# A Flamingo block with two mixture-of-experts layers: the order of the routed tiles, their first rows, the idle shares and the weight blocks rearranged

## The chip, the cores and the metric

The kernel runs on one core of a Trainium2 chip. The metric is the device time of one execution in microseconds (us), the median of several runs; less is better. Engine names: PE is TensorE's matmuls and PEld its weight loads, DVE is VectorE, ACT is ScalarE, POOL is GpSimd, SP is SyncE, which here only issues DMAs.

## The reference, cut to what matters

`x` is 4 x 256 tokens of 256 numbers, so N = 1024 tokens. Four steps follow each other, each with a residual.

```python
x = x + tanh(g_xattn[0]) * L0_xattn(layernorm(x), ctx)          # fp8-quantised product
x = x + tanh(g_ffn[0])   * L0_ffn(layernorm(x), ...)            # 8 small experts, top 2, and a shared one
x = x + tanh(g_xattn[1]) * L1_xattn(layernorm(x), ctx, ctx)     # 16 heads, causal
x = x + tanh(g_ffn[1])   * L1_ffn(layernorm(x), ...)

def L1_ffn(x, rw1, rw2, w1, b1, w2, b2):                        # TOP_K = 2, E = 8, hidden 1024
    probs = softmax(gelu(x @ rw1) @ rw2)
    wgt, idx = top_k(probs, 2)
    for e in range(E):
        Ye = gelu(x @ w1[e] + b1[e]) @ w2[e] + b2[e]
        Ce = gelu(b1[e]) @ w2[e] + b2[e]                        # what a token gets that did not choose e
        for k in range(2):
            mask = idx[..., k] == e
            active = any(mask)
            out = out + active * wgt[..., k] * where(mask, Ye, Ce)
```

The last step holds most of the arithmetic. A token needs `Ye` only for its two experts; for the others it gets a weighted sum of the constant rows `Ce`. The kernel calls that sum the idle share.

## The kernel before, in words

The program is written by hand for each engine: one instruction list per engine, with semaphores between them. Every list runs in order, so an instruction that waits holds up all that stands behind it on its engine. The stages are A (first attention product), B (first expert layer), C (second attention, four batches b = 0 to 3 with twelve pieces u each) and D (second expert layer).

**Weight blocks.** The weights of stage D (`w1`, `w2`, eight experts each) come in 32 blocks of 128 x 1024 numbers, two per expert and matrix, in the order of the list `ORDER`. SP loads block i into staging buffer i % 4 once `s_wlo` says that block i - 4 is done. ACT scales it (L828) and writes its 16-bit high part (L835); POOL then subtracts to get the low part, in four pieces (L663), and raises `s_wlo`. These conversions are laid by hand between the work of stages B to D: `C_BLOCKS` and `SCALE_AT` say which block is scaled at which piece u of stage C (the high part follows at u + 1), `D_BLOCKS` are those left for stage D (blocks 21 to 31; `D_BLOCKS[-2:]` have their low part made by DVE, L2120).

**SP's list in stage C.** Between the loads stand the small DMAs of `load_minus_max(b)` (L516), the rows without which PE cannot begin `scores_by_key(b, 0)` (L1329). `load_minus_max(3)` stands behind the load of block 20.

**Routing.** DVE takes the two largest logits of each token (L2039, L2045), PE counts with matmuls how many tokens before this one chose the same expert, DVE adds up where each expert's run of slots begins, each padded to 128, and makes for each pair (token, choice) a one-hot row of its slot (sixteen instructions, L2080). PE turns them into the list of tokens by slot, DVE stores it as indices (`GI`, `SI`, L2092 to L2094), POOL gathers the rows of a tile from DRAM by them (`gather_rows`, L721).

**Tiles.** There are TILES = 23 tiles of 128 slots. For a tile j: PE transposes its gathered rows (L1528), DVE copies them (`rows_t`, L2127), PE multiplies with the expert's `w1` (`tile_up`, L1544 and L1547, four PSUM banks), DVE adds the halves (`add_halves`, four L2159), ACT does gelu and the high part (L1063, L1070), DVE the low part (`split_hidden`, two L2164), PE multiplies with `w2` (`tile_down`, L1562 and L1565, which stands in the list after `tile_up(j + 1)`), ACT and DVE weight the result (L1078, `tile_out` L2169), POOL adds the rows into DRAM with an indirect accumulating DMA (`add_to_out`, L734). Each `add_to_out` waits until the one before has landed (`s_sc`), and stands in POOL's list behind the gather of tile j + 4, which waits until ACT has copied the row weights of tile j + 2 (`s_ws`, L1057). The expert of a tile is a number read at run time (`EID`); SP copies its `w1` within SBUF into one of three buffers `W1S` (L564) for each tile.

**Idle shares.** PE forms all `Ce` (`idle_outputs`, L1488, 64 matmuls before tile 0 and 64 behind `tile_up(0)`), folds them (L1507), and multiplies with the tokens' coefficients (`idle_shares`, L1516) behind `tile_up(1)`; DVE adds that to X (L2146), SP stores X to `out`, and only then may `add_to_out(0)` run.

## Time and profile before

| what | us |
|---|---|
| median of 3 runs | 435.31 |
| lowest and highest | 434.76 and 436.42 |
| profiled execution, its own time | 430.72 |
| its span, first to last instruction | 428.8 |
| busy in the span: PE, DVE, ACT, POOL | 319.6, 307.7, 262.0, 166.6 |
| mean granted TensorE clock, share of full speed | 0.898 |

The profile is of one execution, whose time is 4.6 us below the median of the timed runs. All times of instructions are from the beginning of its span. A line of a timeline has the start, the duration (of all its instructions together where it ends on xN), engine, line, operation, what is written from what, and in brackets the idle time ahead of it with the engine and line that ended it.

### The profile page before, as it was taken

How to read it: one execution, taken by the hardware profiler on the slowest of the kernel's cores; microseconds unless marked ns; L12 is line 12 of the kernel's file. 1: busy time of each engine (PE TensorE's matmuls, PEld its weight loads, DVE VectorE, ACT ScalarE, POOL GpSimd, SP SyncE). 2: the span in 40 equal slices, each digit the busy share in tenths (PEclk: the TensorE clock that was granted, in tenths of full speed). 3: DMA queues.
4: the chain of work that ended last, by engine and by line, in shares of the span. 5: the costliest groups of instructions: out<-in, count | busy, mean ns of one | idle time of the engine just before them, and what ended most of it. 6: DMA issues, size and time to landing. Idle time of an engine off the chain costs nothing.

```text
span 428.8 us, 8535 instructions
## 1 busy us (share of the span) xinstructions
PE 319.6 (75%) x2638; PEld 216.0 (50%) x2639; DVE 307.7 (72%) x739; ACT 262.0 (61%) x528; POOL 166.6 (39%) x231
## 2 busy tenths in 40 slices
PE   0065988869999968777582511578999999999981
PEld 0054337536477635354341210365777777777760
DVE  3998988863764666759676689466788788888870
ACT  1745656623576476848687598033677777777770
POOL 3041301531284260623671659200355444444422
PEclk9997799989999998979788565678999999999997
DMA  8954000140076073411313535834477777777532
GB/s 265 389 144 136 2 0 2 53 142 2 0 165 233 2 208 72 141 50 51 99 50 99 159 92 147 315 130 171 149 247 248 246 245 245 236 248 233 157 36 24
DMA packets 28097, 60.43 MB, mean 141 GB/s; under 512 B 4401, under 2 KB 19010, under 8 KB 24866
## 3 DMA queue, kind: packets, MB, share of 16 engines
q1 hardware_dynamic: 21186, 52.64, 35.6%
q0 software_dynamic: 4416, 6.13, 8.9%
q10 hardware_dynamic: 2464, 1.27, 1.2%
q8 instruction: 16, 0.26, 0.3%
q14 instruction: 15, 0.12, 0.1%
HBM read 27.43 MB, written 6.32 MB: 79 GB/s over the span
## 4 chain that ended last, share of the span: by engine, by line
DVE 36%; PE 32%; issue 11%; ACT 11%; DMA 4%; POOL 3%; ACTq 1%; DVEq 0%; POOLq 0%
PE bank L1202 6%; PE bank L1544 4%; PE bank L1562 4%; ACT arena L1063 4%; DVE MX L1902 4%; DVE arena L2080 2%; PE bank L1547 2%; PE bank L1163 2%; DVE X L1748 2%; ACT arena L1070 2%; DVE arena L2164 2%; DVE arena L2159 2%; PE bank L1565 2%; DVE stats L1626 2%; ACT arena L945 2%
## 5 line engine op out<-in xcount | busy, mean ns | idle before, releaser
L1063 ACT ACTIVATE arena<-arena,B1D 128x128 f32<-128x128 f32 x184 | 57.6, 392 | 14.3 <-DVE arena L2159 13.7
L1562 PE MATMUL bank<-arena 128*128 x184 | 62.3, 385 | 1.2 <-DVE arena L2164 1.2
L2159 DVE TENSOR_REDUCE arena<-bank 128x256 f32<-128x512 f32 x92 | 57.4, 683 | 4.6 <-PE bank L1547 4.6
L663 POOL TENSOR_TENSOR arena<-STG,arena 128x256 f16<-128x256 f32 x56 | 37.1, 695 | 42.4 <-ACT arena L835 42.4
L663 POOL TENSOR_TENSOR W<-STG,W 128x256 f16<-128x256 f32 x64 | 41.4, 683 | 28.3 <-ACT W L835 28.3
L1565 PE MATMUL bank<-arena 128*128 x184 | 50.7, 276 | 0.0
L734 POOL DMA_INDIRECT out_dram<-arena,SI x23 | 37.3, 1621 | 31.0 <-DMA out_dram<-arena,SI 23.7
L721 POOL DMA_INDIRECT arena<-token_rows,GI x23 | 22.8, 991 | 66.5 <-ACT WS L1057 51.3
L2164 DVE SCALAR_TENSOR_TENSOR arena<-arena 128x512 f16<-128x512 f32 x46 | 29.8, 689 | 24.8 <-ACT arena L1070 24.8
L1544 PE MATMUL bank<-arena 128*128 128x256 f16 x256 | 46.4, 281 | 1.5 <-DVE arena L2127 1.1
L1547 PE MATMUL bank<-arena 128*128 128x128 f16 x256 | 45.4, 225 | 0.0
L945 ACT ACTIVATE arena<-bank 128x512 f32<-128x512 f32 x48 | 27.9, 595 | 22.6 <-PE bank L1332 22.4
L1202 PE MATMUL bank<-arena 128*128 128x256 f32 x160 | 38.8, 395 | 0.5 <-issue 0.5
L828 ACT ACTIVATE STG<-STG 128x1024 f32<-128x1024 f32 x32 | 33.5, 1047 | 6.4 <-DMA STG<-in_l_w_dram 5.0
L1902 DVE TENSOR_REDUCE MX<-bank 128x2 f32<-128x512 f32 (+1 forms) x48 | 31.2, 687 | 8.6 <-PE bank L1304 8.1
L633 POOL TENSOR_TENSOR rstd<-ve,neg_half 128x2 f32<-128x2 f32 (+1 forms) x12 | 9.7, 807 | 68.8 <-DVE ve L1631 68.8
L1202 PEld LDWEIGHTS bank<-arena 128*128 128x128 f32 x160 | 30.4, 196 | 5.5 <-issue 1.5
L1163 PE MATMUL bank<-arena 128*128 128x512 f16 x120 | 31.3, 405 | 0.0
L1544 PEld LDWEIGHTS bank<-arena 128*128 128x128 f16 x256 | 25.8, 101 | 7.5 <-DVE arena L2127 1.3
L1562 PEld LDWEIGHTS bank<-arena 128*128 128x128 f16 x184 | 18.2, 99 | 21.9 <-issue 3.4
L876 ACT ACTIVATE arena<-bank,B1A 128x512 f32<-128x512 f32 x20 | 13.6, 686 | 24.0 <-PE bank L1163 20.1
L1070 ACT ACTIVATE arena<-arena 128x512 f16<-128x512 f32 x46 | 26.1, 613 | 0.0
(266 smaller groups left out, 708.5 us busy)
## 6 DMA issues: line engine op xcount, KB each, us to landing
STG<-in_l_w_dram SPq DMA_DIRECT2D x32, 512.0 KB, 3.6
arena<-W SPq DMA_DIRECT2D x16, 1024.0 KB, 5.0
STG<-W SPq DMA_DIRECT2D x7, 1024.0 KB
arena<-in_l_w_dram SPq DMA_DIRECT2D x2, 1280.0 KB, 12.2
X<-in_x_dram SPq DMA_DIRECT2D x2, 512.0 KB, 6.1
W<-in_ctx_t_dram ACTq DMA_DIRECT2D x2, 512.0 KB, 11.2
W<-in_ctx_dram SPq DMA_DIRECT2D x1, 1024.0 KB, 17.6
k_parts<-W SPq DMA_DIRECT2D x2, 512.0 KB, 3.3
```

Source lines behind the costliest of these rows:

```text
L663: ins = nc.gpsimd.tensor_tensor(l, src, h, ALU.subtract)
L734: pool.indirect_dma_start(out[:, :], bass.IndirectOffsetOnAxis(ap=SI[:, j:j + 1], axis=0), YS[:, j % 2], None, compute_op=ALU.add).then_in ...
L1063: ins = nc.scalar.activation(x, x, ACT.Gelu, bias=B1D[:, e, c:c + 1], scale=1.0 / (X_SCALE * W_SCALE))
L1163: mm = nc.tensor.matmul(bank[UP_BANK[i]][:, :], W1A[:, b, c, k], HT_[:, k, a, h * 512:(h + 1) * 512], start=(n == 0), stop=(n == 5))
L1202: nc.tensor.matmul(dst, GH[:, c, t * P:(t + 1) * P], W2A[:, c], start=(c == 0), stop=False, skip_group_check=True)
L1544: nc.tensor.matmul(o, W1S[r][:, 0, k, c * P:(c + 1) * P], XT[:, q, k].rearrange("p s n -> p (s n)"), start=(k == 0), stop=False, skip_grou ...
L1547: mm = nc.tensor.matmul(o[:, 0:P], W1S[r][:, 1, k, c * P:(c + 1) * P], XT[:, q, k, 0], start=False, stop=(k == KC - 1), skip_group_check=True)
L1562: nc.tensor.matmul(bank[6 + q][:, :], GDL[:, q, 0, c * P:(c + 1) * P], W2[:, e, c].rearrange("p s d -> p (s d)"), start=(c == 0), stop=Fal ...
L1565: mm = nc.tensor.matmul(bank[6 + q][:, 0:D], GDL[:, q, 1, c * P:(c + 1) * P], W2[:, e, c, 0], start=False, stop=(c == HC8 - 1), skip_group ...
L1902: v.tensor_reduce(MX[:, b % 2, i, h0:h0 + nh], s1_bank[n % 2][:, :].rearrange("p (h n) -> p h n", h=nh), AX.X, ALU.max).then_inc(s_mx, 1)
L2159: v.tensor_reduce(half, o, AX.X, ALU.add).then_inc(s_dadd, 1)
L2164: v.scalar_tensor_tensor(out=lo, in0=GD[:, q, hb * 512:(hb + 1) * 512], scalar=G_SCALE, in1=hi, op0=ALU.mult, op1=ALU.subtract).then_inc(s ...
```

## The change

- The first eight tiles are one per expert, in the fixed order `STATIC` = 4, 5, 6, 7, 0, 1, 2, 3. An expert's first 128 tokens go there, whatever the others have; only tokens beyond go to tiles 8 to 22, whose experts are still read at run time. Tiles 0 to 7 take `w1` where it lies, without a copy. All loops over tiles are written out.
- The rows of tiles 0 and 1 are not gathered: DVE makes one-hot rows for them from the rank alone, and PE multiplies them with the rows in SBUF, which gives them transposed. Their gathered rows are still fetched, for the row weights.
- `idle_outputs`, coefficients, fold and `idle_shares` move to behind tiles 6 to 13, with their copies on ACT. X is stored early (`store_base`), and the idle shares are added to `out` by one accumulating DMA of 1 MB (`add_shares`) between `add_to_out(15)` and `add_to_out(16)`. Weighted rows have ten buffers: three for tiles 0 to 15 in turn, and one each for tiles 16 to 22.
- A new order of the weight blocks: ACT splits blocks 4 to 7 before `hidden_gelu(CA)` of stage B; stage C takes blocks 12 to 23, three per batch; blocks 24 to 28 come in stage D before the routing, 29 to 31 after it, with their low parts on POOL between the tiles.

```diff
-        HEAD, UNROLL = 3, 6
+        ONE_HOT = 2
+        STATIC = [*range(E // 2, E), *range(E // 2)]
...
-        C_BLOCKS = [range(10, 13), range(13, 16), range(16, 19), range(19, 21)]
-        SCALE_AT = ((1, 4, 8), (2, 5, 8), (2, 5, 8), (2, 5))
-        D_BLOCKS = range(21, BLOCKS)
+        C_BLOCKS = [range(12, 15), range(15, 18), range(18, 21), range(21, 24)]
+        SCALE_AT = ((5, 8, 10), (2, 5, 8), (2, 5, 8), (2, 5, 8))
+        LATE = 29
+        SHARES_AFTER = 15
+        def weighted(j):
+            return YS[j % 3] if j <= SHARES_AFTER else YS[3 + j - SHARES_AFTER - 1]
+        def added(j):
+            return 16 * (j + 1 + (j > SHARES_AFTER))
...
@@ SP
             load_minus_max(2)
-            for i in range(18, 21):
+            for i in range(21, 25):
                 load_weights(i)
             load_minus_max(3)
...
+            def store_base(h):
+                sp.wait_ge(s_dhs, HT * (h + 1))
+                sp.dma_start(out[h * HT * P:(h + 1) * HT * P, :].rearrange("(t p) d -> p t d", p=P),
+                             X[:, h * HT:(h + 1) * HT, :]).then_inc(s_out, 16)
@@ POOL
-            weights_low(4)
-            pool.wait_ge(s_up, 2 * CA)
-            for i in range(5, 10):
+            for i in range(4, 12):
                 weights_low(i)
...
+            def add_shares(n):
+                pool.wait_ge(s_share, T)
+                pool.wait_ge(s_sc, 16 * n)
+                pool.dma_start(out[0:N, :].rearrange("(t p) d -> p t d", p=P), X[:, :, :],
+                               accum_op=ALU.add).then_inc(s_sc, 16)
...
-            for j in range(4):
+            for j in (2, 0, 3, 1, 4):
                 gather_rows(j)
             for j in range(TILES):
-                if j + 4 < TILES:
-                    gather_rows(j + 4)
+                if j + 5 < TILES:
+                    gather_rows(j + 5)
                 add_to_out(j)
+                if j == SHARES_AFTER:
+                    add_shares(j + 1)
+                if j == 3:
+                    pool.wait_ge(s_gb16, 2)
+                if 3 <= j < 3 + BLOCKS - LATE:
+                    weights_low(LATE + j - 3)
@@ ACT
+            for i in range(4, 8):
+                weights_split(i)
             hidden_gelu(CA)
...
+            def one_hot_rows_out(j):
+                act.wait_ge(s_xt_ps, j + 1)
+                nc.scalar.activation(XT[:, j]..., bank[j][:, :], ACT.Copy).then_inc(s_xt, 1)
+            one_hot_rows_out(0)
+            weights_split(29)
+            one_hot_rows_out(1)
+            for i in range(30, BLOCKS):
                 weights_split(i)
@@ PE
+            def one_hot_rows(j):
+                pe.wait_ge(s_oh, j + 1)
+                for k in range(KC):
+                    for s in range(2):
+                        for t in range(T):
+                            mm = nc.tensor.matmul(bank[j][:, (2 * k + s) * P:(2 * k + s + 1) * P],
+                                                  DHL[:, t, s, k * P:(k + 1) * P], OH[:, j, t], ...)
+                mm.then_inc(s_xt_ps, 1)
...
+            for j in range(ONE_HOT):
+                one_hot_rows(j)
+            for j in range(TILES):
+                e = expert_of(j)
+                tile_up(j, e)
+                if j == 0:
+                    slot_tokens()
+                if 4 <= j + 1 < TILES:
+                    transpose_tile(j + 1)
+                if j:
+                    tile_down(j - 1, e_before)
+                if j in (1, 2):
+                    transpose_tile(j + 1)
+                if j in (6, 7):
+                    transpose_coefficients(j - 6)
+                if j == 8:
+                    idle_outputs()
+                if j == 9:
+                    fold_groups()
+                if j in (10, 11, 12, 13):
+                    idle_shares(2 * (j - 10))
@@ DVE
+            step(v.scalar_tensor_tensor(out=RANK1[:, :, :], in0=rank[:, :, ones_hot], scalar=1.0,
+                                        in1=MSB[:, :, ones_hot], op0=ALU.add, op1=ALU.mult))
+            def one_hot_rows(j):
+                v.tensor_tensor(OH[:, j], iota_1[:, :].unsqueeze(1).broadcast_to([P, T, P]),
+                                RANK1[:, :, j:j + 1].broadcast_to([P, T, P]), ALU.is_equal).then_inc(s_oh, 1)
+            one_hot_rows(0)
...
+            slots_out()
+            for j in range(TILES):
+                add_halves(j)
+                if ONE_HOT <= j + 1 < TILES and j > 2:
+                    rows_t(j + 1)
                 for hb in range(2):
-                    split_hidden(j, j % 2, hb)
+                    split_hidden(j, hb)
+                if j in (1, 2):
+                    rows_t(j + 1)
                 if j:
-                    tile_out(j - 1, (j - 1) % 2)
+                    tile_out(j - 1)
+                if j == 2:
+                    tile_experts()
+                if j == 3:
+                    coefficients()
+                if j == 4:
+                    spread_gelu()
```

## Rows read from the trace of the kernel before

**Rows 1.** The page: the chain that ended last, its shares by engine.

```profile
DVE 36%; PE 32%; issue 11%; ACT 11%; DMA 4%; POOL 3%; ACTq 1%; DVEq 0%; POOLq 0%
```

**Rows 2.** Stretches: length; busy PE, PEld, DVE, ACT, POOL; clock; DMA share; GB/s.

```profile
149.00:161.60 12.60, 8.88 (x116) 5.36 (x116) 7.69 (x21) 9.19 (x17) 7.34 (x11) 0.94 0.66 179
...
207.60:232.70 25.10, 14.58 (x144) 8.37 (x140) 16.68 (x47) 19.76 (x30) 10.45 (x16) 0.84 0.34 101
...
307.00:410.00 103.00, 103.00 (x986) 80.14 (x983) 83.29 (x152) 77.54 (x227) 47.63 (x37) 1.00 0.73 229
```

**Rows 3.** Timeline of DVE from the router's logits to the slots.

```profile
249.09 0.68 DVE L2039 MAX8 DTOP<-bank 128x8 f32<-128x8 f32 x8 [0.55 <-PE bank L1447]
...
256.59 10.06 DVE L2080 TENSOR_SCALAR arena<-iota_p,SMODF,token 128x128 f16<-128x128 f16 x16
...
268.29 0.18 DVE L2094 SCALAR_TENSOR_TENSOR SI<-bank,arena 128x23 uint32<-128x23 f32 x1
...
270.74 2.35 DVE L2120 TENSOR_TENSOR arena<-STG,arena 128x1024 f16<-128x1024 f32 x2
```

**Rows 4.** Timeline of DVE: instructions beside a busy and an idle POOL.

```profile
110.96 0.15 DVE L1638 TENSOR_TENSOR rt<-ve,rstd 128x2 f32<-128x2 f32 x1
...
111.74 0.74 DVE L1886 TENSOR_SCALAR W<-X,mv,rstd 128x256 f32<-128x256 f32 x2
...
237.32 1.40 DVE L1943 TENSOR_SCALAR arena<-X,mv,rstd 128x256 f32<-128x256 f32 x2
```

**Rows 5.** Timeline of POOL: low parts of weight blocks, four pieces a block.

```profile
115.51 2.55 POOL L663 TENSOR_TENSOR W<-STG,W 128x256 f16<-128x256 f32 x4 [10.38 <-ACT W L835]
...
203.38 5.16 POOL L663 TENSOR_TENSOR arena<-STG,arena 128x256 f16<-128x256 f32 x8
```

**Rows 6.** Timelines of ACT and DVE in batch 0 of stage C.

```profile
150.71 1.05 ACT L835 ACTIVATE W<-STG 128x1024 f16<-128x1024 f32 x1
...
158.40 1.56 DVE L1893 TENSOR_TENSOR W<-W 128x256 f16<-128x256 f32 x2 [3.01 <-ACT W L912]
```

**Rows 7.** Timelines of SP and PE where batch 3 begins.

```profile
201.75 1.32 SPq L516 DMA_DIRECT2D arena<-NMS  x2
...
207.59 0.40 PE L1329 MATMUL bank<-ident_b,neg_mask 128*128 128x256 bf16 x1
...
213.58 1.09 PE L1360 MATMUL bank<-ident,arena 128*128 128x128 f32 x4 [3.77 <-DVE arena L1932]
```

**Rows 8.** Timelines of PE (transposes at a low clock) and DVE (one tile).

```profile
183.01 1.04 PE L1280 MATMUL bank<-ident_h,W 128*128 128x128 f16 x8 [1.76 <-DVE W L1893]
...
302.49 2.47 DVE L2159 TENSOR_REDUCE arena<-bank 128x256 f32<-128x512 f32 x4
...
306.35 1.29 DVE L2164 SCALAR_TENSOR_TENSOR arena<-arena 128x512 f16<-128x512 f32 x2 [1.05 <-ACT arena L1070]
...
307.95 2.48 DVE L2159 TENSOR_REDUCE arena<-bank 128x256 f32<-128x512 f32 x4
```

**Rows 9.** Idle outputs in PE's timeline, idle shares in the chain.

```profile
283.41 1.93 PE L1488 MATMUL bank<-arena 128*32 128x256 f16 x64
...
295.22 2.31 PE bank L1516 x8
```

**Rows 10.** Timelines of DVE (tile 17) and POOL (adds of tiles 15, 21, 22).

```profile
384.84 2.48 DVE L2159 TENSOR_REDUCE arena<-bank 128x256 f32<-128x512 f32 x4
...
387.79 1.59 POOL L734 DMA_INDIRECT out_dram<-arena,SI  x1 [0.72 <-issue]
...
418.64 1.55 POOL L734 DMA_INDIRECT out_dram<-arena,SI  x1 [3.04 <-DVE arena L2169]
423.27 1.55 POOL L734 DMA_INDIRECT out_dram<-arena,SI  x1 [3.08 <-DMA out_dram<-arena,SI]
```

**Rows 11.** Waits: who waited for whom, total, times, longest.

```profile
ACT WS L1057 <- DVE arena L2169: 22.1, 21, 1.4
```

**Rows 12.** DMA queue in the last 10.2 us: packets, MB, share of 16 engines.

```profile
q0 software_dynamic: 288, 0.26, 24.1%
```

585 lines of the change are left out of this document (292 added, 293 removed).

## The prediction

> **What bounds the kernel now.** I read the page's chain of waits first. It is shared: DVE 36%, PE 32%, ACT 11% [rows 1], so no engine alone sets the time, and each stage has to be read for itself. The view of busy times by stretch cuts it. In the loop over tiles, 307 to 410 us, PE is busy for all 103 us at full clock, DVE for 80.14 [rows 2]: PE is the bound, and a tile takes 307.95 - 302.49 = 5.46 us [rows 8]. Before it stands a chain of latencies, seen in DVE's timeline: logits at 249.09, sixteen one-hot rows from 256.59 (10.06 us, 0.63 each), the indices done at 268.5 [rows 3], then gathers, transposes, tile 0, idle outputs, idle shares, and the first reduction of tile 3 only at 307.95 [rows 8]. The end is a third regime: POOL's adds wait for the one before to land, 423.27 - 418.64 = 4.63 us apart, and the span ends 5.53 after the last one's issue [rows 10]. In stages B and C, ACT, PE and DVE hand work round, and none is full: ACT is busy 9.19 of 12.60 us in the second half of batch 0 and 19.76 of 25.10 in batch 3 [rows 2].
>
> The profiled span is 428.8, that execution's own time 430.72, the median 435.31. I add the change of the span to the median. The sum has four terms: up to tile 3, extras in the loop, slips in stages B and C, the tail.
>
> **Term 1, up to tile 3: -23.4.** Routing stays where it is up to the ranks. After the last logit (249.1) DVE makes masks, rank and the product RANK1, about as many small instructions as it now does in that time: about 253. The one-hot rows of tile 0 are one instruction on 1024 elements; the nearest price is 2.35/2 = 1.17 us [rows 3], plus some 0.5 because POOL still makes low parts then: 254.8. PE multiplies 32 times at 0.13, the price of the transposes with a slow clock (8 in 1.04) [rows 8]: about 258.5 with its wait. ACT copies, so `tile_up(0)` begins near 261.5 and ends near 264.1. Under this cover DVE makes the second tile's rows (1.2), the slots (thirteen small ones, about 3), and the sixteen one-hot rows for all slots. These took 0.63 each beside a working POOL [rows 3]. DVE instructions are shorter beside an idle one: 0.74 for two `scaled_q` against 1.40 [rows 4]; the shortest small one took 0.15 [rows 4]. POOL has no work here, as its gathers wait for the indices: I take 0.2 each, 3.2 in all, with 0.15 and 0.63 as ends. That puts the slots' end near 264, the indices near 265.5, and the first reduction of tile 0 at 265.5, because it stands behind the indices on DVE. ACT's splits of blocks 29 to 31 end near 266.4 and delay gelu little. From a first reduction to the end of the split a tile takes 306.35 + 1.29 - 302.49 = 5.15 [rows 8]: tile 0 is done at 270.8, tile 1 at 276.1, and with the copy of tile 2's rows (0.4) and its up product (1.1) tile 2 starts at 277.7. Rows are gathered five ahead, so no gather is late. Tile 3 starts at 277.7 + 5.15 + 1.6 = 284.5 instead of 307.95. The idle shares, which separated these tiles, are gone from here, and with them the wait of the first add for the store of X.
>
> **Term 2, extras in the loop: +10.0.** What leaves the front comes back where PE is full. `idle_outputs` cost 1.93 for 64 matmuls, and there are two sets: 3.9. The shares cost 2.31 [rows 9], the fold about 0.6: together 6.8, all on the bound. The coefficients' transposes go to tiles where DVE is late and cost nothing. DVE gets the tiles' experts, the coefficients and the spread of gelu, 3.6 by their count of small instructions, and POOL's low parts of three blocks (2.55 each [rows 5]) stretch DVE's work beside them by up to 0.47 of their time: 7.65 x 0.78 x 0.47 = 2.8. Of these 6.4 the idle time of DVE, (103 - 80.14)/103 x 5.46 = 1.2 per tile [rows 2], over six tiles, can swallow all, if it lies in the right place; I take half, +3.2, with 0 and 6.4 as ends. The W1 copies of tiles 0 to 7 go; they were on no path.
>
> **Term 3, slips in stages B and C: +5.2.**
> (a) POOL's low parts of blocks 4 to 7 move ahead of its wait for stage B's up products and fill a gap of 10.38 us before 115.51 [rows 5]. DVE's `ln_rstd` and `scaled_q` lie in it (four at 0.15, two in 0.74) [rows 4] and stretch by 0.5 and 0.66; PE's maxima wait for them: +1.2, ends 0 and 2.4 (both halves of the rows).
> (b) In batch 0 ACT's six half conversions stand at pieces 5 to 11 instead of 1 to 9, three more in the second half, 1.05 each, in a stretch where DVE once waits 3.01 for ACT [rows 6]. ACT has 3.4 us idle there [rows 2], but in pieces: half of 3.15 is paid, +1.5, ends 0 and 3.15.
> (c) SP's `load_minus_max(3)` is issued at 201.75 now; after, it stands behind the load of block 24, which waits for the low part of block 20, the last of POOL's two blocks from 203.38 (5.16): 208.5 [rows 5]. With issue (1.32 for its two) and landing PE could begin `scores_by_key(3, 0)` near 212.9 instead of 207.59 [rows 7]. PE has 3.77 us of idle time soon behind that [rows 7], which covers part: 5.3 - 3.8 = +1.5, ends 0 and 2.5.
> (d) Batch 3 gets one more block, 2.1 on ACT, of whose 5.3 idle us [rows 2] not all can be used: +1.0, ends 0 and 2.1.
> At nothing: the splits of blocks 4 to 7 ahead of stage B's gelu (ACT is idle there and gelu is used some 5 us later), the early store of X (SP, behind the token rows), five gathers ahead, static experts (fewer register loads, on queues that wait anyway). If ACT's cover in stage B is gone, a split costs 2 us each.
>
> **Term 4, the tail: +5.7.** Now: from the first reduction of tile 17 (384.84) to the end are 43.96 us, with the add of tile 15 issued 2.95 later, at 387.79 [rows 10]; the row weights' wait for `tile_out` [rows 11], which ten buffers remove, is part of that. After: add 15 at +1.3, 4.63 for its landing, then `add_shares`, D, then six gaps of 4.63, then 5.53: 39.2 + D. Behind this 1 MB transfer stand on POOL adds 16 to 22 and gathers 21 and 22. No row shows a transfer of this kind and size. Its floor is one add, 4.63. Two adds of 128 KB used 24.1% of 16 engines over 10.2 us [rows 12], 1.23 us of all engines each; eight times that is 9.8, and with the fixed 3.4 of an add 13.2. Direct rows should be somewhat cheaper than indirect ones: D = 10.5, so 49.7 - 43.96 = +5.7. The tail is as long as now at D = 4.7. The other six buffers only let ACT and DVE run ahead.
>
> **Sum.** -23.4 + 10.0 + 5.2 + 5.7 = -2.5: span 426.3, time 435.3 - 2.5 = 432.8 us. Most of the gain at the front is paid back in three other places, so the sum is small beside its terms.
>
> **Rivals.** 0.5%, or 2.2 us, is about what a measurement can tell from no change.
> 1. The share add is short (faster). Only its landing counts, and at D = 4.7 term 4 is zero: 432.8 - 5.8 = 427.1. For it: two adds in the tail leave 16 engines three quarters idle [rows 12], so an add's time is mostly latency, not data. Against: eight times the packets. Chance 0.19. The Trainium skill's page "DMA: Bandwidth & Descriptors", section "Anatomy of one DMA - SWDGE (gpsimd) path", is on this rival's side: it gives a GpSimd transfer a fixed 2.0 us plus its bytes at 436 GB/s, an estimate of 4.4 us for 1 MB; by it the sum would be rival 1's. No row of before has a transfer of this size with accumulation; the indirect adds' 4.63 for 128 KB is above the page's 2.3.
> 2. ACT and POOL find room for all moved conversions (faster): term 3 is zero, 427.6. For it: ACT has idle time in each batch [rows 2]. Against: DVE's wait for ACT in batch 0 [rows 6]. Chance 0.10.
> 3. They find none: term 3 is at its upper ends, 10.1, so 437.7. Chance 0.13.
> 4. The share add is long (slower). An indirect add keeps POOL for 1.59 us to build 128 rows' descriptors [rows 10]; eight times as many is 12.7, and if the data follow partly behind, D is 16 (landing alone behind) to 25, say 20: +9.5, 442.3. It makes the kernel slower from D = 10.5 + 2.5 + 2.2 = 15.2. For it: nothing can pass it, as the next add waits for its landing. Against: plain rows need no index each. Chance 0.15.
> 5. The early tiles don't come early, because the sixteen one-hot rows stay at 0.63 (not POOL but their form was what cost): 16 x 0.43 = +6.9, 439.7. Chance 0.11.
> My forecast holds 0.32.
>
> **How the numbers follow.** The likeliest is the sum, 432.8. Its own range is 429 to 436.5. The wanted range takes in rivals 1 and 2 (427) with half of the other small terms, and rivals 3, 5 and the lower half of 4: 425.5 to 443. Outside are rivals 1 and 2 together and a share add over 20 us. Faster by over 0.5%: rivals 1 and 2 (0.29) and the half of the forecast below 433.1 (0.17): 0.46. Slower: 4, 5 and half of 3: 0.32. Same: 0.22.
>
> **What would show it.** From the last logit to the first reduction of tile 3 should take 35.5 us instead of 58.9, the sixteen one-hot rows about 3 instead of 10. From tile 3 to tile 15 there should be about 10 us more than thirteen times 5.46. PE's first scores of batch 3 should begin 5 us later after its predecessor, and DVE should wait longer for ACT in batches 0 and 3. The gap between POOL's adds 15 and 16 should be 4.6 + 10.5, the later adds 4.63 apart. I am wrong if tile 3 still waits for DVE's slots (term 1), if the loop stays at 5.46 per tile with the extras in it (term 2), if the router's logits come no later than 249 (term 3), or if the gap around the share add is under 10 or above 20 us (term 4).

## The result: slower, by what was lost ahead of the router

The changed kernel takes 440.34 us (median of 4 runs, 439.03 to 441.44) against 435.03 for the kernel before in the same session: ratio 1.0125, 95% interval 1.0072 to 1.0178. Ratios are taken over the fast runs of each kernel, those within 1.5% of its fastest, so below they are not always the quotient of the medians. The forecast was 432.8, faster; the time lies in the forecast's range and on the other side. The profiled span grew from 428.8 to 437.3, by 8.5 us, while the medians are 5.3 apart: the profiled execution of before was a short one (430.72 against its median of 435.03), the one of the changed kernel less so (439.03 against 440.34). The 8.5 is nearer to what is usual: in two later groups the kernel before had medians of 430.94 and 431.12, and the nearest stand-ins for the changed kernel, e1 and e5 below, 440.71 and 440.43, with ratios of 1.027. The working below is on the two spans.

Four markers cut both traces where the forecast cut them.

| stretch | before | changed | difference | forecast |
|---|---|---|---|---|
| start to the router's logits (first MAX8) | 249.09 | 258.36 | +9.3 | +5.2 |
| logits to the first reduction of tile 3 | 58.86 | 33.17 | -25.7 | -23.4 |
| tile 3 to tile 17 | 76.89 | 91.26 | +14.4 | +10.0 |
| tile 17 to the end | 43.96 | 54.51 | +10.5 | +5.7 |
| span | 428.8 | 437.3 | +8.5 | -2.5 |

From the logits to the end the change is worth 0.8 us (179.7 against 178.9). What it gains at the first tiles is paid back, all but 0.8 us, by the loop and the tail, and what it loses in stages B and C is the loss.

The page's chain that ended last, where DMA has risen from 4% [rows 1] to 15%:

```profile
PE 31%; DVE 30%; DMA 15%; ACT 12%; issue 8%; POOL 2%; SPq 0%; ACTq 0%; DVEq 0%; POOLq 0%
```

DVE of the changed kernel from the logits to tile 3. L2200 are the sixteen one-hot rows (L2080 of before), L2256 a tile's reductions (L2159), L2262 the split's low parts (L2164).

```profile
258.36 0.68 DVE L2136 MAX8 DTOP<-bank 128x8 f32<-128x8 f32 x8 [0.55 <-PE bank L1528]
...
261.82 1.56 DVE L2160 TENSOR_TENSOR arena<-iota,RANK 128x1024 f16<-128x1024 f16 x1
...
269.01 3.65 DVE L2200 TENSOR_SCALAR arena<-iota_p,SMODF,token 128x128 f16<-128x128 f16 x16
...
273.48 2.47 DVE L2256 TENSOR_REDUCE arena<-bank 128x256 f32<-128x512 f32 x4
...
285.02 2.57 DVE L2256 TENSOR_REDUCE arena<-bank 128x256 f32<-128x512 f32 x4 [0.64 <-PE bank L1652]
...
291.53 2.57 DVE L2256 TENSOR_REDUCE arena<-bank 128x256 f32<-128x512 f32 x4
```

This is what the change was built for, and it works: the sixteen rows take 3.65 us instead of 10.06 [rows 3], tile 0 starts 15.1 us after the logits, and three tiles later the loop runs at 291.53 instead of 307.95 [rows 8].

The loop. DVE's splits in tiles 5, 6, 7 and 8, while POOL makes the low parts of blocks 29 to 31 in the first three:

```profile
308.29 4.33 DVE L2262 SCALAR_TENSOR_TENSOR arena<-arena 128x512 f16<-128x512 f32 x2 [0.97 <-ACT arena L1122]
...
316.70 2.32 DVE L2262 SCALAR_TENSOR_TENSOR arena<-arena 128x512 f16<-128x512 f32 x2 [0.97 <-ACT arena L1122]
...
323.11 1.77 DVE L2262 SCALAR_TENSOR_TENSOR arena<-arena 128x512 f16<-128x512 f32 x2 [0.97 <-ACT arena L1122]
...
329.06 1.29 DVE L2262 SCALAR_TENSOR_TENSOR arena<-arena 128x512 f16<-128x512 f32 x2 [1.07 <-ACT arena L1122]
```

PE's idle outputs, fold, and the first of four calls of the idle shares:

```profile
328.18 3.68 PE L1582 MATMUL bank<-arena 128*32 128x256 f16 x128
...
338.22 0.61 PE L1603 MATMUL bank<-arena,fold 128*16 128x256 f32 x2
...
344.32 1.12 PE L1611 MATMUL bank<-arena 24*128 24x256 f32 x4
```

In the kernel before a tile takes 5.49 us here (76.89 for 14). Tiles 3 to 8 take 33.7 us, 6.2 more than five times 5.49; tiles 8 to 10 3.6 more than two times (outputs and fold), tiles 10 to 14 4.5 more than four times (1.1 for each call of the shares). The three make the 14.4.

The tail, on POOL: the add of tile 15, the share add (L751), the gather of tile 21 behind it, the add of tile 16, and the last add.

```profile
386.33 1.59 POOL L744 DMA_INDIRECT out_dram<-arena,SI  x1 [1.20 <-DMA out_dram<-HV,SI]
391.85 1.70 POOL L751 DMA_DIRECT2D out_dram<-X  x1 [3.93 <-DMA out_dram<-arena,SI]
393.86 1.09 POOL L735 DMA_INDIRECT arena<-token_rows,GI  x1 [0.30 <-issue]
404.62 1.65 POOL L744 DMA_INDIRECT out_dram<-arena,SI  x1 [9.67 <-DMA out_dram<-X]
409.27 1.58 POOL L744 DMA_INDIRECT out_dram<-arena,SI  x1 [1.29 <-DMA out_dram<-arena,SI]
...
432.06 1.56 POOL L744 DMA_INDIRECT out_dram<-arena,SI  x1 [3.00 <-DMA out_dram<-arena,SI]
```

The share add takes 404.62 - 391.85 = 12.77 us in the chain of adds. The chain that ended last runs over these transfers from the add of tile 12 on (start, length):

```profile
368.69 5.82 DMA out_dram<-arena,SI
...
391.85 11.99 DMA out_dram<-X
...
404.62 3.87 DMA out_dram<-arena,SI
...
427.50 3.81 DMA out_dram<-arena,SI
```

What the 16 DMA engines did while the share add ran, from 391.8 to 404.7 (queue, packets, MB, share of their time; then the gather of tile 21 with its us to landing):

```profile
q0 software_dynamic: 1088, 1.18, 59.1%
q1 hardware_dynamic: 280, 2.04, 40.5%
...
arena<-token_rows,GI POOLq DMA_INDIRECT x1, 11.1
```

They were busy nearly all the time: q0 is the share add with the gather behind it, q1 the copies of `w1` for the run-time tiles. The gather landed after 11.1 us, so tile 21 starts 5.7 us late (its first reduction comes 11.2 us after that of tile 20, not 5.5). That is not on the chain, as its add waits still longer for the adds ahead.

Stages B and C. First DVE: its scaling of rows beside POOL's moved low parts, and its wait for ACT in batch 0:

```profile
113.03 1.40 DVE L1983 TENSOR_SCALAR W<-X,mv,rstd 128x256 f32<-128x256 f32 x2
...
162.49 1.27 DVE L1990 TENSOR_TENSOR W<-W 128x256 f16<-128x256 f32 x2 [5.45 <-ACT W L937]
```

Then PE: maxima late behind DVE, and the first scores of batch 3, which wait for the rows of `load_minus_max(3)`:

```profile
115.68 0.39 PE L1381 MATMUL bank<-neg_mask,ident_b 128*128 128x512 bf16 x1 [1.63 <-DVE MX L1999]
...
215.76 0.40 PE L1410 MATMUL bank<-ident_b,neg_mask 128*128 128x256 bf16 x1 [4.54 <-DMA arena<-NMS]
```

And SP, which issues these rows behind the load of block 24:

```profile
187.53 24.87 SPq L480 DMA_DIRECT2D STG<-in_l_w_dram  x4
212.44 1.31 SPq L531 DMA_DIRECT2D arena<-NMS  x2
```

By the same instructions in both traces (PE's first scores of batch 0, then DVE's additions of the hidden keys' share `HV` to the finished values, of which there are two a batch and which stand in the list one batch later) the 9.3 us are, rounded: +1.7 up to the first scores of batch 0, +2.3 in batch 0, -0.5 in the next two batches, +1.5 from there to the values that are finished as batch 3 begins, +3.3 in batch 3, +0.9 in the router.

### The profile page after: what moved, and what is told of

Its sections match the earlier page's. It is cut to its first block, busy times and chain, and to the rows that moved or that the text cites. A ratio compares the mean times of both kernels' runs of the same rounds, so it can differ in the third digit from the quotient of the medians.

```text
span 437.3 us, 7969 instructions
## 1 busy us (share of the span) xinstructions
PE 325.1 (74%) x2694; PEld 219.9 (50%) x2694; DVE 301.0 (69%) x729; ACT 265.7 (61%) x541; POOL 177.6 (41%) x242
## 3 DMA queue, kind: packets, MB, share of 16 engines
q0 software_dynamic: 5456, 7.18, 10.2%
## 4 chain that ended last, share of the span: by engine, by line
PE 31%; DVE 30%; DMA 15%; ACT 12%; issue 8%; POOL 2%; SPq 0%; ACTq 0%; DVEq 0%; POOLq 0%
DMA out_dram<-arena,SI 9%; PE bank L1283 6%; DVE MX L1999 4%; ACT arena L1115 4%; PE bank L1668 3%; DMA out_dram<-X 3%; PE bank L1649 3%; DVE arena L2262 2%; DVE X L1845 2%; DVE stats L1723 2%; ACT arena L860 2%; ACT arena L970 2%; PE bank L1244 2%; DMA W<-in_ctx_t_dram 2%; PE bank L1558 1%
## 5 line engine op out<-in xcount | busy, mean ns | idle before, releaser
L1668 PE MATMUL bank<-arena 128*128 (+1 forms) x184 | 62.7, 386 | 2.9 <-DVE arena L2262 2.6
L2256 DVE TENSOR_REDUCE arena<-bank 128x256 f32<-128x512 f32 x92 | 57.7, 682 | 7.6 <-PE bank L1652 7.6
L676 POOL TENSOR_TENSOR arena<-STG,arena 128x256 f16<-128x256 f32 x64 | 47.3, 839 | 35.8 <-ACT arena L860 35.8
L1671 PE MATMUL bank<-arena 128*128 (+1 forms) x184 | 51.0, 277 | 0.0
L2262 DVE SCALAR_TENSOR_TENSOR arena<-arena 128x512 f16<-128x512 f32 x46 | 34.3, 786 | 24.2 <-ACT arena L1122 24.2
L744 POOL DMA_INDIRECT out_dram<-arena,SI x18 | 28.6, 1588 | 37.9 <-DMA out_dram<-arena,SI 21.6
L1668 PEld LDWEIGHTS bank<-arena 128*128 128x128 f16 x184 | 18.2, 99 | 23.7 <-issue 3.6
L1649 PE MATMUL bank<-arena 128*128 128x256 f16 x160 | 27.5, 273 | 1.1 <-issue 0.8
L1652 PE MATMUL bank<-arena 128*128 128x128 f16 x160 | 26.9, 219 | 0.0
L1649 PE MATMUL bank<-arena,W 128*128 128x256 f16 x128 | 22.0, 273 | 6.5 <-DVE arena L2243 5.2
L1410 PE MATMUL bank<-ident_b,neg_mask 128*128 128x256 bf16 (+1 forms) x48 | 16.5, 345 | 13.2 <-ACT arena L970 8.6
L735 POOL DMA_INDIRECT arena<-token_rows,GI x16 | 16.8, 1053 | 23.3 <-ACT WS L1102 20.3
```

What stands on the lines that cost most here:

```text
L676: ins = nc.gpsimd.tensor_tensor(l, src, h, ALU.subtract)
L1649: nc.tensor.matmul(o, w1[:, 0, k, c * P:(c + 1) * P], XT[:, q, k].rearrange("p s n -> p (s n)"), start=(k == 0), stop=False, skip_group_ch ...
L1668: nc.tensor.matmul(bank[6 + q][:, :], GDL[:, q, 0, c * P:(c + 1) * P], W2[:, e, c].rearrange("p s d -> p (s d)"), start=(c == 0), stop=Fal ...
L1671: mm = nc.tensor.matmul(bank[6 + q][:, 0:D], GDL[:, q, 1, c * P:(c + 1) * P], W2[:, e, c, 0], start=False, stop=(c == HC8 - 1), skip_group ...
L2256: v.tensor_reduce(half, o, AX.X, ALU.add).then_inc(s_dadd, 1)
L2262: v.scalar_tensor_tensor(out=lo, in0=GD[:, q, hb * 512:(hb + 1) * 512], scalar=G_SCALE, in1=hi, op0=ALU.mult, op1=ALU.subtract).then_inc(s ...
```

## The experiments

All start from the changed kernel. They ran in three groups, each on one chip and with its own runs of the kernel before; the medians of before differ from group to group (430.94, 431.12 and 433.22 us, against 435.03 above), so times are compared within a group, and stretches of the traces by markers. Two stretches vary between executions. The logits of the variants that change nothing ahead of them came between 257.35 and 259.33. From the logits to the end the changed kernel, e1, e9, e5 and e12, whose code behind the logits is the same, took 178.9, 180.6, 178.9, 181.7 and 180.5 us, most of it the share add (11.4 to 13.8 us). A gain at the end that is read from one pair of traces is not known to better than 2 to 3 us.

### The first group: SP's order, the share add, its place, POOL's low parts

**e1_minus_max**

```diff
-            for i in range(21, 25):
+            for i in range(21, 24):
                 load_weights(i)
             load_minus_max(3)
```

> The changed kernel with one thing put back: SP issues load_minus_max(3) ahead of the load of block 24, not behind it. In the trace of the changed kernel these two small DMAs are issued at 212.44 although ACT has written their rows at 205.2, and PE waits 4.5 us for them. Theory (the stage slips because SP's queue order holds PE): they are issued near 205.3, PE's wait of 4.5 us goes, and the logits come 2 to 4.5 us earlier than 258.36, the whole kernel as much. Rival (PE's wait only stands ahead of another one, for DVE or ACT, which then lasts longer): the first scores of batch 3 come 4.5 us earlier, but the logits less than 1 us.

Measured: 440.71 us, ratio 1.0272 (1.0157 to 1.0388). The edit missed its aim: SP issued the rows at 211.20, only 1.2 us earlier, since the load of block 23 ahead of them waits as well, and PE still waited 2.88 us for them. The stretch up to the values at the beginning of batch 3 was already down to 13.1 us, as in e9 below. Behind that the run is the changed kernel, and serves as the stand-in for it in this group.

**e2_no_share_add**

```diff
-            return 16 * (j + 1 + (j > SHARES_AFTER))
+            return 16 * (j + 1)
...
-                if j == SHARES_AFTER:
-                    add_shares(j + 1)
```

> The changed kernel without the accumulating transfer of the idle shares: the shares are computed, but not added to out (the output lacks them). Theory (the chain of adds sets the end, and the transfer stands in it with its 12.8 us): without it the adds follow the tiles, tile 22 has its first reduction near 410, its add near 418.5, the end near 424.5, 12 to 13 us less than the 437.3 of the changed kernel's span. Rival (the loop itself is late, PE at its bound, and the chain of adds only follows): under 5 us less.

Measured: 429.56 us, 11.2 below e1; ratio to before 1.0019 (0.9962 to 1.0077). The span is 427.6, 9.7 less than 437.3. The theory holds, with a price of 9.5 us from the logits to the end by this pair of traces and 11.2 by the medians, where the transfer itself took 12.8 in the changed kernel and 13.3 in e1. POOL's adds of tiles 15 and 16 and the last one:

```profile
385.58 1.59 POOL L744 DMA_INDIRECT out_dram<-arena,SI  x1 [1.17 <-DMA out_dram<-HV,SI]
392.69 1.59 POOL L744 DMA_INDIRECT out_dram<-arena,SI  x1 [2.84 <-DMA out_dram<-arena,SI]
...
422.22 1.55 POOL L744 DMA_INDIRECT out_dram<-arena,SI  x1 [2.95 <-DMA out_dram<-arena,SI]
```

Without the transfer the adds still wait for one another: the seven steps from tile 15 to tile 22 take 36.6 us, 5.2 each, not 4.6. The chain of adds sets the end with the share add and without it.

**e3_share_after_12**

```diff
-        YS = [at(110.25, [D], F32), at(111.25, [D], F32), HV[:, 0]] + [at(96 + i, [D], F32) for i in range(7)]
+        YS = [at(110.25, [D], F32), at(111.25, [D], F32), HV[:, 0]] + [at(96 + i, [D], F32) for i in range(10)]
-        SHARES_AFTER = 15
+        SHARES_AFTER = 12
```

> The changed kernel with the share add after the add of tile 12 instead of tile 15, and 13 buffers for weighted rows instead of 10. Theory (in the chain of adds a tile's add takes 4.6 us where PE needs 5.5 a tile, so three tiles more behind the transfer win back three times 0.9 and what the chain lags at tile 15): span 437.3 - 2.7 - 1.5, about 433. Rival (the transfer gets longer where more copies of w1 run beside it, or its accumulation hits gathers that PE needs): no gain, 436 to 439.

Measured: 441.67 us, 1.0 above e1, ratio 1.0296 (1.0179 to 1.0414); span 437.9. The rival's time holds, no gain, and not its first reason: the transfer did not get longer. The share add and the adds of tiles 13, 14 and 22:

```profile
375.20 1.68 POOL L751 DMA_DIRECT2D out_dram<-X  x1 [5.26 <-issue]
387.61 1.64 POOL L744 DMA_INDIRECT out_dram<-arena,SI  x1 [9.33 <-DMA out_dram<-X]
393.26 1.58 POOL L744 DMA_INDIRECT out_dram<-arena,SI  x1 [2.54 <-DMA out_dram<-arena,SI]
...
432.36 1.56 POOL L744 DMA_INDIRECT out_dram<-arena,SI  x1 [2.93 <-DMA out_dram<-arena,SI]
```

The transfer took 12.4, the nine steps behind it 44.75, 4.97 each: beside copies of `w1` and gathers an add takes nearly what PE takes for a tile (5.5), so that three more tiles behind the transfer win almost nothing. The theory had 4.6, which makes 3.3 us of its miss over nine steps; 1.4 more are the 7.0 us from the add of tile 12 to the transfer, where the changed kernel had 5.5 behind the add of tile 15.

**e4_no_lows** (the products of blocks 29 to 31 lack the low part)

```diff
-                    weights_low(LATE + j - 3)
+                    pool.wait_ge(s_whi, LATE + j - 2)
+                    nc.gpsimd.memset(weight_block(LATE + j - 3)[2], 0.0).then_inc(s_wlo, 1)
```

> The changed kernel with POOL's low parts of blocks 29 to 31, which stand between the adds of tiles 3 to 5, replaced by a clearing of the same memory (one short instruction a block; their products lack the low part). Theory (these subtractions hold DVE up: its two split instructions take 4.33, 2.32 and 1.77 us beside them instead of 1.29, and DVE is then the bound): tiles 5 to 8 come at 6.1 us each instead of 8.43, 6.40 and 5.86, and the loop is 3 to 4.5 us shorter up to tile 8; at the end as much is left, as the chain of adds follows the loop. Rival (DVE has slack there, or PE's idle outputs wait for something else): under 1 us.

Measured: 435.99 us, 4.7 below e1, ratio 1.0169 (1.0052 to 1.0285); span 433.8. DVE's splits in tiles 5 and 6:

```profile
307.35 1.29 DVE L2263 SCALAR_TENSOR_TENSOR arena<-arena 128x512 f16<-128x512 f32 x2 [0.96 <-ACT arena L1123]
...
312.73 1.29 DVE L2263 SCALAR_TENSOR_TENSOR arena<-arena 128x512 f16<-128x512 f32 x2 [0.97 <-ACT arena L1123]
```

They are back at 1.29 and the tiles at 5.4 us. By markers from the logits tile 8 is 4.6 us earlier than in the changed kernel, which is what the three splits there took over 1.29 (4.33 + 2.32 + 1.77 - 3.87 = 4.55); tile 10 and the add of tile 15 are 3.3 earlier, the end 2.7. The theory holds for the loop up to tile 8. The loop itself gives 1.3 back where the idle outputs and the fold stand (9.08 and 6.78 us from tile 8 to 10, instead of 8.42 and 6.11). How much arrives is not settled: 2.7 by the two traces, 4.7 by the medians.

### The second group: stage C, POOL at the one-hot rows, the copies

**e9_minus_max_22**

```diff
-            for i in range(21, 25):
+            for i in range(21, 23):
                 load_weights(i)
             load_minus_max(3)
-            for i in range(25, 28):
+            for i in range(23, 28):
```

> The changed kernel with load_minus_max(3) issued on SP behind the load of block 22. (In the first try it stood behind the load of block 23, which itself waited for the low part of block 19 until 211.2, so it came only 1.2 us earlier; that run tells nothing of this wait.) Theory (SP's order holds PE): issued near 206, PE's wait of 4.5 us for these rows goes, the logits come 2 to 3.5 us earlier, and the end, which the chain of adds hands on one to one, as much. Rival (another wait lasts longer instead): under 1 us.

Measured: 438.38 us, ratio 1.0211 (1.0096 to 1.0326); e5 below, whose logits hardly moved, had 440.43. SP issued the rows at 206.12, PE's wait for them is gone, and this stands in its place:

```profile
217.98 1.09 PE L1441 MATMUL bank<-ident,arena 128*128 128x128 f32 x4 [4.44 <-DVE arena L2029]
```

So the rival is half right: PE now waits 4.44 us for DVE, as it waited 3.77 before [rows 7]. By the markers the stretch up to the values at the beginning of batch 3 went from 14.6 back to 13.1 us, its length in the kernel before: the wait cost 1.5, and not 4.5. The logits, at 257.31, are 1.1 earlier than in the changed kernel, no more than two executions differ by.

**e5_stage_c**

```diff
-        SCALE_AT = ((5, 8, 10), (2, 5, 8), (2, 5, 8), (2, 5, 8))
+        SCALE_AT = ((2, 5, 8), (2, 5, 8), (2, 5, 8), (2, 5, 8))
...
             for i in range(4, 12):
+                if i == 6:
+                    pool.wait_ge(s_hc, 4)
                 weights_low(i)
```

> The changed kernel with two edits in stages B and C: POOL waits before the low part of block 6 until DVE has scaled the rows of batch 1, and ACT scales the blocks of batch 0 at pieces 2, 5 and 8 as in the other batches, not at 5, 8 and 10. Theory (POOL beside DVE costs 1.3 us at 111 and the late conversions cost 2.9 us in batch 0): the scaling starts at 111.8 instead of 113.0 and takes 0.74 instead of 1.40, batch 0 begins near 136.8 instead of 138.4, batch 1 near 162.5 instead of 166.4, of which 1 us is lost again by batch 3: logits 2.5 to 3.5 us earlier, the end the same. Rival (the conversions cost the same wherever they stand, POOL's later low parts hold up the loads): under 1 us, or later.

Measured: 440.43 us, ratio 1.0268 (1.0152 to 1.0383); logits at 257.88. Half of it held. DVE's scaling:

```profile
112.06 0.74 DVE L1985 TENSOR_SCALAR W<-X,mv,rstd 128x256 f32<-128x256 f32 x2
```

On ACT, the first conversion of batch 0:

```profile
149.99 1.06 ACT L855 ACTIVATE STG<-STG 128x1024 f32<-128x1024 f32 x1 [6.09 <-PE bank L1288]
```

With POOL held back the scaling takes 0.74 again, PE's 1.63 us wait is gone, and the first scores of batch 0 come at 137.54 instead of 138.27, in a run whose earlier work was 0.3 later: 1.1 of the 1.7 us come back. The conversions show why batch 0 cannot get its 2.3 us back: block 12 goes where stage B's last products still read, so at piece 2 ACT waits for them until 149.99, and batch 0 is as long as before the edit (29.7 us from the first scores to the values here and in the changed kernel, 27.3 before).

**e7_busy_pool**

```diff
+            for i in range(20):
+                pool.wait_ge(s_busy, i + 1)
+                nc.gpsimd.tensor_tensor(BUSY[:, 1], BUSY[:, 0], BUSY[:, 0], ALU.subtract).then_inc(s_busy, 1)
             pool.wait_ge(s_rows, 16 * 3)
```

> The changed kernel with POOL kept busy by twenty subtractions on spare memory, of the size of the low parts, ahead of its first gathers. Theory (the sixteen one-hot rows take 0.23 us each here and took 0.63 before because POOL was idle here and busy there): they take 0.6 to 0.63 again, near 10 us instead of 3.65, the indices come 6 us later, and so do tile 0 and the end. Rival (the price comes from the order or the memory of the rows, not from POOL): they stay at 0.23, and only the gathers come a little later, the end under 2 us later.

Measured: 448.05 us, 7.6 above e5; ratio 1.0464 (1.0358 to 1.0571). The sixteen rows on DVE:

```profile
271.96 6.04 DVE L2206 TENSOR_SCALAR arena<-iota_p,SMODF,token 128x128 f16<-128x128 f16 x16
```

The rows take 0.38 us each instead of 0.23 (2.4 us in all), the small instructions ahead of them take 2.3 more, and tile 0 starts 19.8 us after the logits instead of 15.1. The size is not the 0.63 of the kernel before, and the single rows say why (count, then shortest, median and longest in ns; this run, then the kernel before):

```profile
L2206 DVE TENSOR_SCALAR arena<-iota_p,SMODF,token x16: 301/452/604, 272.0 to 277.7; 128x128 f16<-128x128 f16 x16
...
L2080 DVE TENSOR_SCALAR arena<-iota_p,SMODF,token x16: 657/706/709, 256.6 to 265.9; 128x128 f16<-128x128 f16 x16
```

Here a row of 0.60 and one of 0.30 take turns, and two rows go by in 0.75 us, the step of POOL's subtractions, which have a gap of 0.08 after each. In the kernel before the subtractions are back to back, 0.63 us apart, and so are the rows, from the second on each starting at most 0.02 us behind a subtraction. So the rows keep step with POOL, one or two to a subtraction, and the price is POOL's: the rival is out. What is lost here arrives at the end: tile 3 is 6.2 us later from the logits, a part of it because the gathers stand behind the subtractions, and the end 6.4.

**e8_no_copies** (tiles 8 to 22 use the expert j mod 8)

```diff
-                return pe.value_load(EID[0:1, j:j + 1], min_val=0, max_val=E - 1)
+                return j % E
...
-                    pe.wait_ge(s_w1s[(j - E) % 3], 16 * ((j - E) // 3) + 16)
-                    w1 = W1S[(j - E) % 3]
+                w1 = W1[:, e]
...
-            for j in range(E, TILES):
-                load_tile_weights(j)
```

> The changed kernel without the copies of w1 for tiles 8 to 22: these tiles take the expert (number of the tile) mod 8, where its w1 lies (the output is not the reference's). Theory (the copies, 1 MB a tile, share the 16 DMA engines with the adds; they were 40% of the engines' time under the share add): the share add takes 8 to 10 us instead of 12.8, the adds behind it stay at 4.6, those ahead of it land faster (15 to share 4.6 instead of 5.5), and the end comes 4 to 6 us earlier. Rival (the share add is bound by its own 1024 packets of 1 KB with accumulation): it stays above 12 us and the end moves by under 2 us.

Measured: 432.39 us, 8.0 below e5, ratio 1.0084 (1.0037 to 1.0131); span 429.0. POOL's add of tile 15, the share add, the add of tile 16:

```profile
381.12 1.60 POOL L742 DMA_INDIRECT out_dram<-arena,SI  x1 [0.30 <-issue]
385.59 1.70 POOL L749 DMA_DIRECT2D out_dram<-X  x1 [2.88 <-DMA out_dram<-arena,SI]
...
396.09 1.65 POOL L742 DMA_INDIRECT out_dram<-arena,SI  x1 [7.40 <-DVE arena L2261]
```

The share add among the DMA issues (KB, us from issue to landing):

```profile
out_dram<-X POOLq DMA_DIRECT2D x1, 1024.0 KB, 9.7
```

The share add is 10.5 us to the next add without copies beside it, a little above the theory's 8 to 10 and well under the rival's 12, and it is issued 4.5 us behind the add ahead of it instead of 5.5. The theory holds, and the gain is more than it asked. Not all of it is the chain's: by markers from the logits tile 9 is 2.4 us earlier than in the changed kernel (the splits beside POOL's low parts take 7.1 us in three tiles instead of 8.4, and the outputs cost less), the add of tile 15 4.2, the add of tile 16 7.5, the end 7.3. So some 5 us are the chain of adds, and behind the share add nothing is won. The register reads of the experts' numbers, which go with the copies, are not the reason: tiles 10 to 17 keep their 6.6 and 5.5 us.

### The third group: PE's share, an early share add, block 23

**e6_few_idle** (96 of the 128 matmuls of the idle outputs left out)

```diff
-                    for c in range(HC8):
+                    for c in (0, HC8 - 1):
```

> The changed kernel with 32 of the 128 matmuls of the idle outputs (two of eight chunks of the hidden units; the constant rows are incomplete). Theory (the loop is PE's, and what is put into it costs its full time, and the chain of adds hands it on to the end): tile 8 to tile 9 takes 5.7 us instead of 8.4, and the end comes 2.5 to 3 us earlier. Rival (the chain of adds sets the pace from earlier on, so that PE's time up to tile 12 is covered): tile 9 comes earlier, the end under 1 us.

Measured: 438.14 us, ratio 1.0227 (1.0121 to 1.0333); span 437.6 with logits 1.0 later than in the changed kernel. By markers from the logits tile 9 comes 2.8 us earlier than in the changed kernel and the add of tile 12 2.9 us earlier, but the share add's end 1.4 and the end 0.6. Up to the add of tile 12 the theory holds: the outputs' time is PE's, and the adds hand it on. By this pair of traces the chain of adds behind it swallows most of the gain, as the rival says; but the five other executions with the same tail spread over 2.8 us, and against the longest of them the end is 3.4 earlier. The run does not settle it, and neither does the median, as no unedited kernel ran in this group.

**e10_early_shares**

```diff
-        SHARES_AFTER = 15
+        SHARES_AFTER = 9
-            return YS[j % 3] if j <= SHARES_AFTER else YS[3 + j - SHARES_AFTER - 1]
+            return YS[j % 3] if j <= SHARES_AFTER else YS[3 + (j - SHARES_AFTER - 1) % 10]
...
             for j in (2, 0, 3, 1, 4):
                 gather_rows(j)
+            for i in range(LATE, BLOCKS):
+                weights_low(i)
...
-                if j == 8:
+                if j == 5:
                     idle_outputs()
```

> The changed kernel with everything of the idle shares three tiles earlier and the share add behind the add of tile 9 instead of 15: low parts of blocks 29 to 31 on POOL right behind the first five gathers, coefficients, spread and tile experts on DVE behind tiles 1 to 3, idle outputs behind tile 5, shares behind tiles 7 to 10, ten buffers in a ring for tiles 10 to 22. Theory (the share add costs its 12.8 us because at tile 15 the chain of adds has no slack left; from tile 9 on, 13 more adds can win some of it back, at 5.0 us each against PE's 5.5): the first add behind the transfer comes near 367, twelve more at 5.0, the end near 432, 5 to 6 us before the 437.3 of the changed kernel. Rival (adds beside the copies of w1 take as long as PE takes for a tile, so that no place wins anything back; the share add after tile 12 gave 437.9): 436 to 438.

Measured: 439.24 us, 1.1 above e6; ratio 1.0262 (1.0154 to 1.0369); span 438.0. The share add in the chain that ended last (start, length, transfer):

```profile
356.79 13.90 DMA out_dram<-X
```

The rival's time holds again, and not quite its reason. The transfer is on the chain at tile 9 as at tiles 12 and 15; twelve steps behind it took 61.5 us, 5.1 each, near the theory's 5.0 and under PE's 5.5. What the theory missed is the first add behind the transfer, which came at 371.5 and not near 367: the transfer took 14.7 us to the next add, and it was issued late, as with POOL's low parts ahead of the loop tiles 3 to 8 start 3.7 us later from the logits than in the changed kernel. So this run shows no gain, but it does not test the place of the transfer alone. The gather behind the transfer is late here too: tile 15 starts 6.2 us late, as tile 21 does by 5.7 in the changed kernel and tile 18 by 5.5 in e3.

**e12_block_23**

```diff
-        C_BLOCKS = [range(12, 15), range(15, 18), range(18, 21), range(21, 24)]
-        SCALE_AT = ((5, 8, 10), (2, 5, 8), (2, 5, 8), (2, 5, 8))
+        C_BLOCKS = [range(12, 15), range(15, 18), range(18, 21), range(21, 23)]
+        SCALE_AT = ((5, 8, 10), (2, 5, 8), (2, 5, 8), (2, 5))
...
-            for i in range(24, 27):
+            for i in range(23, 27):
                 weights_split(i)
```

> The changed kernel with block 23 split after batch 3 (with blocks 24 to 26), as before, instead of inside batch 3. Theory (the third block in batch 3 costs ACT 2.1 us in a stretch where the others wait for it, and is the largest part of what batch 3 lost, 3.3 us; behind batch 3 ACT waits 4.09 us for DVE, so there it is free): the logits come 2 to 3 us earlier, the end the same. Rival (batch 3 is longer for another reason, POOL's order or SP's): under 0.7 us.

Measured: 436.12 us, 2.0 below e6; ratio 1.0181 (1.0072 to 1.0290). Batch 3 is 3.0 us shorter by its markers (16.4 instead of 19.4; 16.1 before), and behind it ACT, with one block more, still waits for DVE:

```profile
243.17 0.42 ACT L982 ACTIVATE arena<-arena 128x256 f16<-128x256 f32 x1 [1.61 <-DVE arena L2040]
```

The theory holds, with the logits 3.6 us earlier (254.77): the third block is what batch 3 lost, and behind the batch it is free.

**e13_all**

The edits of e10, e9, e12 and the hold of e5 at once.

> The early share add, load_minus_max(3) behind the load of block 22, POOL's hold before block 6, and block 23 after batch 3, all at once. If the single effects add up (5.5, 1.4, 1, 2.5), the span is near 427, against 437.3 of the changed kernel and 428.8 of the one before. If the chain of adds has no slack anywhere, only what lies ahead of the loop counts: 432 to 433.

Measured: 435.30 us, 2.8 below e6; ratio 1.0166 (1.0055 to 1.0276), span 434.6, nearer to the second case (432 to 433) than to the sum (427). The logits come at 254.71, 3.7 earlier than in the changed kernel, and the end 2.7. The single effects do not add up: the logits are no earlier than with the edit of e12 alone (254.77), as batch 3 takes 17.6 us here and 16.4 there, and the early share add wins nothing. Of these edits only the one of block 23 shows at the end, and no version that computes the whole layer beats the kernel before.

## Why the prediction was wrong

The step that failed is the pricing of the moved work: in terms 2 and 3 it got the middle of its bounds, as the engines had idle time in these stretches, and the idle time covered nearly nothing; in term 2 half of the idle shares' matmuls were left out besides; in term 4 the share add was priced as if no copies ran beside it, in a chain of adds that was taken to keep up with the tiles. Terms 2, 3 and 4 came out 4.4, 4.1 and 4.8 us above their forecast. That the time lies in the range is no credit to the sum: its own range was 429 to 436.5, and only the room for rivals 3 to 5 reached 440.

**What bounds the kernel.** Right in its three regimes, wrong in two points. The 80.14 us given to DVE in the loop are those of the weight loads; DVE's are 83.29 [rows 2], so its idle time was 1.0 us a tile and not 1.2, which changes no term, as half of 6.4 was taken anyway. And the loop was called PE's alone: the adds were priced with the 4.63 of the end [rows 10], where no copies run. Beside the copies a step of the chain took 5.0 to 5.2 us (e2, e3, e10), so against PE's 5.5 it wins back 0.3 to 0.5 us a tile, and not 0.9.

**Term 1, up to tile 3 (-23.4 forecast, -25.7 measured).** Right step by step: tile 0 starts 15.1 us after the logits where 16.4 was forecast, the sixteen rows take 3.65 where 3.2 was taken, and the end moves with them (e7). Rival 5 is out: e7 shows the rows in step with POOL's subtractions.

**Term 2, the loop (+10.0, measured +14.4).** PE's part was 8.1 instead of 6.8. The outputs were right (3.68 against 3.9). The shares were mis-sized by a reading error: the row of 2.31 us in the chain [rows 9] held 8 matmuls, and there are 16; four calls at 1.12 make 4.5. DVE's part was 6.2, near the upper end of 6.4, not the middle of 3.2. The 47% by which DVE was to be slowed beside POOL came from `scaled_q` [rows 4]; the split took 4.33 instead of 1.29, and e4 puts 4.6 us of the 6.2 on the three blocks. DVE's idle time per tile, which was to swallow half, is waits inside the tile's own chain (0.97 for ACT ahead of each split), and covers nothing: tiles 5 to 7 take the 5.38 us of e4 and all that their splits grew by.

**Term 3, stages B and C (+5.2, measured +9.3).** Each place that was named gave way, and so the list was right and its sizes were not: (a) 1.7 for 1.2, (b) 2.3 for 1.5, (c) 1.5 for 1.5, (d) 3.3 for 1.0, and 0.9 in the router that was not foreseen. The step that failed is to give each the middle of its bounds because an engine had idle time in the stretch: ACT's 5.3 idle us in batch 3 [rows 2] covered nothing of the third block, and (d) went over its upper end of 2.1, the block's own time. e12 shows (d), e5 gives back 1.1 us of (a), e9 shows (c); (b) is read from DVE's wait for ACT alone (5.45 instead of 3.01 [rows 6]), and e5 shows why an earlier place did not help.

**Term 4, the tail (+5.7, measured +10.5).** The mechanism was right: the share add stands in the chain of adds, and nothing passes it (e2). D was 12.8, not 10.5. The working from the row of two adds [rows 12] had given 13.2, and I went below it because direct rows should be cheaper, which no row or run shows; that e8 has just 10.5 is chance. But e8 shows what was missing in the sum, the copies of `w1` beside the transfer, which take 40% of the DMA engines' time and are not in the row. The add of tile 15 was issued 3.5 us after tile 17's first reduction, not 1.3, because it waits for the adds ahead of it, and the share add followed 5.5 us behind it instead of 4.6. These are 2.3, 2.2 and 0.9 us; the rest of the tail was 0.6 shorter than forecast.

**The rivals.** Rival 1, a short share add, is out. The Trainium skill's page "DMA: Bandwidth & Descriptors", section "Anatomy of one DMA - SWDGE (gpsimd) path", by which it took an estimated 4.4 us, does not fit this transfer: with accumulation into 1 KB rows and no copies beside it, it landed 9.7 us after its issue (e8). Rival 2 is out, rival 3 came true in its sum (9.3 of its 10.1) and not in its parts, as (a) to (c) stayed under their ends and (d) and the router went over, and rival 4 did not (D under 15.2, and POOL needed 1.70 us to issue, not 12.7). The result is the forecast's own mechanisms with terms 2, 3 and 4 above their middles together: 4.4, 4.1 and 4.8 us more, less 2.3 by which term 1 gained more, on a sum that was only -2.5.

**What stays open.** Why the router takes 0.9 us more, why the third block costs batch 3 more than its own 2.1 us, where a share add would cost least, and how much of a gain in the loop gets past the chain of adds (by traces 2.7 of 4.6 us in e4 and 0.6 of 2.8 in e6, by medians 4.7 in e4).

## What to carry to other kernels

When a change brings a certain gain in one place and moves work into others, do not price the moved work at the middle of its bounds because the engines there have idle time on average; if its place hands work from engine to engine, take at least the work's own duration (the third block cost 3.3 us for its 2.1), and count all its instructions, not those that the chain happens to show. A chain of transfers that wait for one another has the rate it shows beside the other traffic, not the rate of its quiet end, and a long transfer put into it cost some 10 of its 13 us here, with nothing won at any of the three places tried. Ask of each early gain whether what ends the kernel starts earlier with it; here it did, and was then made longer by as much.

## What the runs showed that was not expected

- DVE's two low parts of a split beside POOL's subtractions: 4.33 us instead of 1.29, more than three times as long, where `scaled_q` only doubled. Nearly all of it is the second one, 3.21 us long, which ended 0.6 us behind the last of POOL's four.
- DVE's one-hot rows keep step with POOL's subtractions: one row to each where these are back to back, two where a gap of 0.08 us stands between them.
- An accumulating transfer of 1 MB in 1 KB rows, from its issue to that of the next add: 10.5 us without copies within SBUF beside it, 11.4 to 15.3 with them; a gather issued behind it landed after 11.1 us with the copies and 8.0 without.
- PE can wait 4.5 us for a small DMA that stands in the wrong place of a queue, and its removal be worth 1.5, because DVE's next result is nearly as late.
